# Expert counts as a row on every partition, and their running sums by accumulating VectorE passes

## What is computed

```python
x = x + gnn(layernorm(x), adj, ...)          # dense attention, masked by adj
...
logits = xf @ Wr + br                        # 2048 x 64
topk_logits, topk_idx = jax.lax.top_k(logits, 2)
gates = jax.nn.softmax(topk_logits, axis=1)
combine = zeros((T, E)).at[arange(T)[:, None], topk_idx].add(gates)
for e in range(64):
    h = relu(xf @ W1[e] + b1[e])             # hidden width 256
    y = h @ W2[e] + b2[e]
    out = out + combine[:, e:e + 1] * y
x = x + out
```

## Time and profile before

| what | us |
|---|---|
| median of 3 runs | 273.82 |
| lowest and highest run | 273.25, 275.77 |
| the profiled execution, span from first to last instruction | 278.2 |
| of it: attention stage, about | 17 to 132 |
| last routing and the plan, about | 132 to 167 |
| expert stage, about | 167 to 262 |

### The profile page before, as it was taken

How to read it: one execution, slowest core, us unless ns; L and a number is a source line. 1 busy time by engine, 2 the same in 40 slices (tenths; PEclk the granted TensorE clock), 3 DMA queues, 4 the chain that set the end, 5 groups by cost and what they waited for, 6 DMA issues and landing times.

```text
span 278.2 us, 6188 instructions
## 1 busy us (share of the span) xinstructions
PE 221.1 (79%) x1849; PEld 211.8 (76%) x1849; DVE 219.3 (79%) x628; ACT 173.6 (62%) x393; POOL 167.4 (60%) x194
## 2 busy tenths in 40 slices
PE   1493998989677878869933369999999999999840
PEld 1263998989677877869933249999999999999740
DVE  6899999999999999998866413889887666666464
ACT  2758777978665868658415025878876777777400
POOL 5770007163788588888667344445888888866600
PEclk9998699999999999979995556999999999999995
DMA  6989744876649607019911122222149710100067
GB/s 157 202 164 171 139 76 75 194 194 184 164 85 252 224 26 294 31 26 375 416 45 48 36 57 57 61 66 72 51 133 319 252 40 31 40 28 24 31 199 262
DMA packets 11119, 36.88 MB, mean 133 GB/s; under 512 B 2256, under 2 KB 2832, under 8 KB 10320
## 3 DMA queue, kind: packets, MB, share of 16 engines
q0 software_dynamic: 5232, 14.98, 24.6%
q1 hardware_dynamic: 5424, 21.11, 21.7%
q10 hardware_dynamic: 432, 0.40, 0.6%
HBM read 39.36 MB, written 5.51 MB: 161 GB/s over the span
## 4 chain that ended last, share of the span: by engine, by line
PE 45%; DVE 33%; issue 9%; DMA 5%; another core or an unknown queue 2%; ACT 1%; POOL 1%; SPq 1%; ACTq 1%; POOLq 0%; DVEq 0%
PE bank L1117 17%; PE bank L1129 15%; DVE arena L721 8%; DVE arena L727 7%; PE bank L1015 4%; PE bank L999 3%; DVE arena L712 3%; DMA arena<-result 2%; DMA xs<-in_x 2%; DVE xs L735 2%; DVE st L738 2%; PE bank L1106 1%; DVE xs L808 1%; DVE idx L758 1%
## 5 line engine op out<-in xcount | busy, mean ns | idle before, releaser
L1015 PE MATMUL bank<-arena 128*128 128x130 f32 x512 | 62.7, 279 | 1.9 <-ACT arena L569 1.9
L1015 PEld LDWEIGHTS bank<-arena 128*128 128x128 f32 x512 | 60.4, 194 | 2.6 <-DVE xs L735 1.5
L1117 PE MATMUL bank<-arena 128*128 x384 | 61.3, 284 | 0.6 <-ACT arena L623 0.5
L1129 PE MATMUL bank<-w2s,arena 128*128 x384 | 59.2, 277 | 0.2 <-issue 0.2
L425 POOL DMA_INDIRECT table<-rows_in,pos x32 | 48.0, 1501 | 11.4 <-issue 8.1
L1117 PEld LDWEIGHTS bank<-arena 128*128 128x128 f32 x384 | 52.0, 197 | 1.4 <-issue 1.3
L1129 PEld LDWEIGHTS bank<-w2s,arena 128*128 128x128 f32 x384 | 51.2, 194 | 0.6 <-issue 0.6
L891 DVE SCALAR_TENSOR_TENSOR arena<-bank,arena 128x128 f32 x96 | 33.6, 350 | 22.2 <-PE bank L1129 15.2
L628 ACT ACTIVATE arena<-bank,arena 128x128 f32<-128x128 f32 x96 | 35.2, 367 | 19.8 <-PE bank L1117 15.4
L999 PE MATMUL bank<-ident,arena 128*128 128x128 f32 x256 | 33.8, 290 | 13.9 <-DVE arena L727 13.9
L999 PEld LDWEIGHTS bank<-ident,arena 128*128 128x128 f32 x256 | 30.5, 149 | 15.1 <-DVE arena L727 15.1
(11 more groups left out here) (193 smaller groups left out, 273.9 us busy)
## 6 DMA issues: line engine op xcount, KB each, us to landing
arena<-in_adj POOLq DMA_DIRECT2D x16, 512.0 KB, 5.4
w2s<-in_w SPq DMA_DIRECT2D x8, 768.0 KB, 4.9
arena<-in_w SPq DMA_DIRECT2D x6, 1024.0 KB
arena<-in_w SPq DMA_DIRECT2D x4, 512.0 KB
w2s<-in_w SPq DMA_DIRECT2D x4, 512.0 KB
xs<-in_x SPq DMA_DIRECT2D x4, 256.0 KB, 6.5
arena<-result SPq DMA_DIRECT2D x2, 512.0 KB, 4.3
arena<-result SPq DMA_DIRECT2D x4, 256.0 KB, 6.1
```

What stands on the lines that cost most here:

```text
L1015: ins = pe.matmul(OB[t % 2][:, 0:D + 2], pt_r[:, t % 2, j, :], h[:, j, :], start=(j == 0), stop=(j == T - 1))
L1117: ins = pe.matmul(hp(p, b), w1u[:, p % UW, P * b:P * b + P], xT_all[:, bass.ds(column, P)], start=True, stop=True)
L1129: ins = pe.matmul(yp(p), hT[:, p % UH, b, :], w2s[:, bass.ds(u, 1), b, :].rearrange("p e d -> p (e d)"), start=(b == 0), stop=(b == HB - 1))
```

## The change

The counts are no longer a column with one partition per expert. PE multiplies `ones` (128 x 128) with each `both` matrix, so that all 128 partitions hold the same row of 64 counts (`tally`, in PSUM bank 0). A first product with `tiny` adds the half. Nine of the ten products need only the groups 0 to 5 and stand ahead of the wait for the last group; the last one stands between that wait and `route_c(6)`.

With the row on every partition, DVE makes the running sums itself. It rounds the row (`paired`, 64 x 64), and passes over it twice, once with a mask of the experts below (`below_f`) and once with those up to this one (`upto_f`). Each pass multiplies and accumulates along the row into one column of `blocks_to`. The three products L1077 to L1079 and the two waits around them are gone. The marks come from `blocks_to` by a few instructions on one or two columns. `place(6)` is split into `gates(6)`, which stays ahead of the plan, and `slots(6)`, which now stands behind the plan's first part. The expert's own count for `pad_at` is picked from the row by a third accumulating pass (`mine`), also behind it. POOL makes the two masks at the start of the kernel with a memset and two selects, in place of three copies.

```diff
             top2(6)
-            place(6)
+            gates(6)
...
             dve.wait_ge(s_tp, 1)
-            dve.tensor_scalar(halves[:, :], M0[0:E, 0:1], 0.5, MAGIC, ALU.mult, ALU.add).then_inc(s_half, 1)
-            dve.tensor_scalar(pad_at[:, :], M0[0:E, 0:1], first_row[:, :], None, ALU.add).then_inc(s_pad, 1)
+            dve.tensor_scalar(paired[:, :], tally[0:E, :], 0.5, MAGIC, ALU.mult, ALU.add).then_inc(s_half, 1)
             dve.wait_ge(s_half, 1)
-            dve.tensor_scalar(edge[0:E, :], halves[:, :], MAGIC, 2.0 / P, ALU.subtract, ALU.mult).then_inc(s_edge, 1)
-            dve.tensor_scalar(c_e, halves[:, :], 2.0, -2.0 * MAGIC, ALU.mult, ALU.add)
-            dve.tensor_scalar(side_e, halves[:, :], 2.0, P - 2.0 * MAGIC, ALU.mult, ALU.add)
-            dve.tensor_scalar(w_e, halves[:, :], -1.0, MAGIC + STRIDE // 2, ALU.mult, ALU.add).then_inc(s_num, 1)
-
-            dve.wait_ge(s_tp, 2)
-            dve.tensor_scalar(mark[:, :], ends, MAGIC, None, ALU.add).then_inc(s_mark, 1)
-            dve.wait_ge(s_mark, 1)
+            dve.scalar_tensor_tensor(skip[:, :], paired[:, :], MAGIC, below_f[:, :], ALU.subtract, ALU.mult,
+                                     accum_out=blocks_to[:, 0:1]).then_inc(s_to, 1)
+            dve.wait_ge(s_to, 1)
+            dve.scalar_tensor_tensor(skip[:, :], paired[:, :], MAGIC, upto_f[:, :], ALU.subtract, ALU.mult,
+                                     accum_out=blocks_to[:, 1:2]).then_inc(s_to, 1)
+            dve.wait_ge(s_to, 2)
+            dve.tensor_scalar(last_exact[:, :], blocks_to[:, 1:2], 0.5, (1.0 - P) * 0.5 / P, ALU.mult, ALU.add).then_inc(s_last, 1)
+            dve.tensor_scalar(mark[:, 0:2], blocks_to[:, :], (2.0 - P) * 0.5 / P, MAGIC, ALU.add, ALU.add).then_inc(s_mark, 1)
+            dve.tensor_scalar(c_e, blocks_to[:, 1:2], blocks_to[:, 0:1], float(P), ALU.subtract, ALU.mult).then_inc(s_num, 1)
+            dve.wait_ge(s_last, 1)
+            dve.tensor_scalar(last_g, last_exact[:, :], MAGIC, None, ALU.add).then_inc(s_mark, 1)
             dve.wait_ge(s_num, 1)
-            dve.scalar_tensor_tensor(frac[:, :], last_g, MAGIC, ends[:, 2:3], ALU.subtract, ALU.subtract).then_inc(s_frac, 1)
+            dve.tensor_scalar(w_e, c_e, -0.5, float(STRIDE // 2), ALU.mult, ALU.add).then_inc(s_num, 1)
+            dve.tensor_scalar(side_e, c_e, float(P), None, ALU.add).then_inc(s_num, 1)
+            dve.wait_ge(s_mark, 2)
+            dve.scalar_tensor_tensor(frac[:, :], last_g, MAGIC, last_exact[:, :], ALU.subtract, ALU.subtract).then_inc(s_frac, 1)
...
             dve.tensor_scalar(in_block, part[:, :], frac[:, :], None, ALU.is_le).then_inc(s_where, 1)
 
+            slots(6)
+            dve.wait_ge(s_to, 2)
+            dve.scalar_tensor_tensor(skip[:, :], tally[0:E, :], 1.0, ident[0:E, 0:E], ALU.mult, ALU.mult,
+                                     accum_out=mine[:, :]).then_inc(s_mine, 1)
+            dve.wait_ge(s_mine, 1)
+            dve.tensor_scalar(pad_at[:, :], mine[:, :], first_row[:, :], None, ALU.add).then_inc(s_pad, 1)
+
+            dve.wait_ge(s_num, 3)
             dve.tensor_scalar(r_blk[0:E, :], pair_of, last_e, None, ALU.is_gt)
...
             route_c(5)
-            route_c(6)
...
-            total = earlier(NG)
-            for n, c in enumerate(total):
-                pe.matmul(M0[0:E, 0:1], c, ones[:, 0:1], start=(n == 0), stop=False)
-            pe.matmul(M0[0:E, 0:1], ones_f[0:1, 0:E], half[:, :], start=False, stop=True).then_inc(s_tp, 1)
+            pe.matmul(tally, ones[:, :], tiny[:, :], start=True, stop=False)
+            for c in earlier(NG - 1):
+                pe.matmul(tally, ones[:, :], c, start=False, stop=False)
+            pe.wait_ge(s_both, NG)
+            pe.matmul(tally, ones[:, :], both[:, SLOT[NG - 1], :], start=False, stop=True).then_inc(s_tp, 1)
+            route_c(6)
             pe.wait_ge(s_tri, 1)
-            pe.wait_ge(s_edge, 1)
-            pe.matmul(ends[:, 0:1], before_f[:, :], edge[:, :], start=True, stop=True)
-            pe.matmul(ends[:, 1:2], upto_f[:, :], edge[:, :], start=True, stop=True)
-            pe.matmul(ends[:, 2:3], upto_h[:, :], edge[:, :], start=True, stop=True).then_inc(s_tp, 1)
             pe.wait_ge(s_where, 1)
```

More of the change, by code:

```diff
@@ L120, in build @@
         ones_f = sb("ones_f", [E, P])
-        before_f, upto_f, upto_h = (sb(f"{k}_f", [E + 1, E]) for k in ("before", "upto", "upto_half"))
+        below_f, upto_f, skip = (sb(f"{k}_f", [E, E]) for k in ("below", "upto", "skip"))
+        paired = sb("paired", [E, E])
+        tiny = sb("tiny", [P, E], BF16)
         steps_i = sb("steps_i", [P, TAB + NB + NG2], I32)
@@ L133, in build @@
         sidx = sb("sidx", [P, 1])
-        halves = sb("halves", [E, 1])
+        mine = sb("mine", [E, 1])
+        blocks_to = sb("blocks_to", [E, 2])
+        last_exact = sb("last_exact", [E, 1])
         turn_e = sb("turn_e", [E, 1])
-        edge = sb("edge", [E + 1, 1])
         mark = sb("mark", [E, 3])
@@ L181, in build @@
         LB, RB = [M0] * (NG - 1) + [bank[1]], [M1] * (NG - 1) + [bank[2]]
-        ends, coded, sides, b1_at = bank[0][0:E, 0:3], bank[4][0:1, 0:2 * WORDS], bank[5], bank[3][:, 0:HB * TAB]
+        tally, coded, sides, b1_at = bank[0][:, 0:E], bank[4][0:1, 0:2 * WORDS], bank[5], bank[3][:, 0:HB * TAB]
         d_x = [sem(f"d_x{i}") for i in range(4)]
@@ L428, in _ @@
             load(4)
[L429 to L431 removed]
+            pool.memset(skip[:, :], 2.0 / P).then_inc(s_skip, 1)
+            pool.wait_ge(s_skip, 1)
+            pool.affine_select(out=below_f[:, :], in_=skip[:, :], compare_op=ALU.is_gt, fill=0.0,
+                               base=0, pattern=[[-1, E]], channel_multiplier=1)
+            pool.affine_select(out=upto_f[:, :], in_=skip[:, :], compare_op=ALU.is_ge, fill=0.0,
+                               base=0, pattern=[[-1, E]], channel_multiplier=1)
             pool.tensor_scalar(part[:, :], iota_p[0:E, :], -1.0 / P, ROUND, ALU.mult, ALU.add)
@@ L689, in _ @@
                 dve.memset(radix[E:E + 1, j:j + 1], 64.0 ** j)
[L690 to L694, removed]
+            dve.memset(tiny[:, :], 0.5 / P)
             dve.memset(padrow[:, :, :], 0.0).then_inc(s_set, 1)
-            dve.wait_ge(s_pool, 4)
+            dve.wait_ge(s_pool, 3)
             dve.wait_ge(s_set, 1)
@@ L767, in top2, with gates @@
                 dve.tensor_tensor(both[:, kept(q), :], hot[:, 0, kept(q), :], hot[:, 1, kept(q), :], ALU.add).then_inc(s_both, 1)
-            def place(q):
+            def gates(q):
                 n = SIZE[q]
@@ L776, in place, with slots @@
                 dve.tensor_tensor(gate[:, 1, rows], ge[:, 0:n], gate[:, 0, rows], ALU.mult).then_inc(s_gate, 1)
+            def slots(q):
+                n = SIZE[q]
+                rows = slice(START[q], START[q + 1])
                 dve.wait_ge(s_rk, q + 1)
@@ L786, in place @@
                                          rank[:, :, 0:n], ALU.mult, ALU.add).then_inc(s_pos, 1)
+            def place(q):
+                gates(q)
+                slots(q)
             def base(q):
```

20 lines of the change are left out of this document (10 added, 10 removed).

## The result

| | kernel before | changed kernel |
|---|---|---|
| median, us | 273.81 (15 runs, 272.79 to 275.77) | 275.51 (15 runs, 274.30 to 276.45) |
| ratio to before, 95% interval | | 1.005 [1.0027, 1.0074] |
| span of the profiled execution, us | 278.2 | 273.9 |
| its own time, us | not shown | 275.76 |

The changed kernel is slower by half a per cent, 0.7 to 2.0 us (1.4 by the ratio, 1.70 between the medians). The forecast was 274.2, with 74% for "within 1%". The two spans must not be compared: the one of before holds late turns that its repetition doesn't have (first experiment).

What follows compares the result with a forecast made beforehand. POOL's queue of writes, with landing and gathers, was taken to bound the experts' start. With prompt PE-to-DVE turns, 0.3 for the later first product plus 0.1 for slower writes on 273.82 gave 274.2 us (58%), range 269.5 to 275.6.

Steps and rivals of the forecast that it cites:

- late turns: Waits from PE to DVE ahead of L841, L850 and group 4's L779 in the first trace: 2.55, 2.20 and 1.05 us.
- The late turns are not in the runs: PE-to-DVE turns: 5.8 us of lateness belongs to the profiled execution only; without it the first L1117 starts at 162.1.
- The plan's chain, 2.4 us: DVE from the counts to s_where: 2.4 us (1.8 to 3.4), s_where 5.9 earlier than in the first trace.
- The writes slip by 1.1: POOL's last writes wait for the last s_pos at 152.7, though POOL is free at 151.6.
- 0.7 of it is hidden by ACT: Start of the expert stage: ACT's 0.7 us of slack takes up part of the slip of POOL's writes.
- the 0.3 of the sum: First expert product L1117: at 162.4 in place of 162.1, so 0.3 us later.
- 0.1 for writes beside DVE's plan: POOL's last writes, now beside DVE's plan, add 0.1 us (median write 1026 ns, best 957).
- the 6.2 us: Skill rule: a profile's total lies 6.2 us above the reported time; by it the runs would be 272.0, late waits included.
- What gives or takes in this stage shifts the end one for one: Stage between 141 and 168 us: its gains or losses shift the expert stage and the end by the same amount.
- may differ by a microsecond: PE's clock in the expert stage: its return may differ by a microsecond, counted in the forecast's own range 273.2 to 275.4.
- That late turns were in the runs: Two rivals on PE-to-DVE waits: 269.6 us if tally comes promptly (14%), 271.9 us if it is late too (18%).
- The third rival: slots(6) behind the plan becomes the bound through the last s_pos; 276.6 us with counts 2.4 late; chance 8%.

Runs made afterwards that it cites:

- first experiment: The kernel before, unchanged, run and profiled once more: 273.86 us, ratio 0.9996; the profiled execution took 272.53 us with a span of 270.6.
- the two experiments that close or narrow POOL's gap: Changed kernel with the last group's places ahead of the plan again, 274.48 us; changed kernel with the padding write ahead of the last tile's two writes, 274.71 us.
- the ten transposes: Kernel before with ten extra PE transposes, result unused, ahead of its first take: 274.60 us, ratio 1.0023.
- the padding first: Changed kernel with mine and pad_at ahead of the marks and POOL's padding write ahead of the last tile's two writes: 274.71 us, ratio 1.0026.
- the places first: Changed kernel with the places of the last group (L781 to L790) ahead of the plan again: 274.48 us, ratio 1.0021.
- the kernel before with its loads first: Kernel before with PE's register loads ahead of its last plan products, b1p in another bank and copied later: 276.93 us, ratio 1.0108.
- the changed kernel with transposes: Changed kernel with seventeen extra PE transposes, result unused, ahead of its first take: 274.82 us, ratio 1.0037.
- the last kernel with its loads first: Changed kernel with places ahead of the plan, PE's register loads ahead of its last plan products, one POOL write ahead of tile 14's rstd: 276.40 us, ratio 1.0089.
- the kernel before with its queue earlier: Kernel before with one tile 10 write ahead of tile 14's rstd and ACT's b1p copy behind its first w1 copies: 273.98 us, ratio 0.9993.

## Why the prediction was right, and which term was off

- *The late turns are not in the runs.* Right, as far as it can be seen: the repeated profile, of a run of 272.53 us, has none of them, and its first product comes 21.55 behind tile 15's residual, where I had 162.1 - 141.1 = 21.0.
- *The plan's chain, 2.4 us.* Right: 2.16. Over PE, with the prompt turns of the repeated profile, it is 2.36, so the passes gain 0.2 us; most of the 5.9 us that the prediction read from the first profile were its late turns.
- *The writes slip by 1.1.* Right in the main: 1.04, and the two experiments that close or narrow POOL's gap give back 1.03 and 0.80 us. The 1.1 counts from the moment when POOL is free; between the prediction's own starts (padding at 155.25 against 154.4) lie 0.85, and its later times go by that.
- *0.7 of it is hidden by ACT.* The size is off (the prediction's own times give 0.55), and the cover is another one. In the kernel before the first take starts at 159.74, 5.06 behind the end of L872 at 154.68; the register loads last about that long (5.05 with the ten transposes, which need no gather; 5.2 when moved). Its gather was issued at 156.37; with the 2.94 us from issue to take of the changed kernel (158.02 to 160.96) it was there at 159.31, an estimate. So PE's loads hid some 0.43 of the slip. The experts start 0.68 later, against the 0.3 of the sum. The first product came at 162.66, where I had 162.4.
- *0.1 for writes beside DVE's plan.* Wrong by that much: 0.96 us each, as the others. With that, the rule of the Trainium skill, "SBUF — State Buffer", section "Who interferes with whom", that VectorE can keep GpSimd from writing its descriptors, shows no trace in these two writes. The long writes of the earlier trace rows lie in the attention stage (2.23 us at 122.81 and 2.94 at 125.35 in the repeated profile); what held them up was not tested. Nor do the runs show the 6.2 us of the Trainium skill, "Runtime: NRT & Kernel Launch", section "The ~15µs preamble/postamble breakdown": where a run's time and span are both given, the time lies above the span, by 1.86 us in the changed kernel (275.76 and 273.9). These spans end with the last instruction, so the total that the section speaks of is not among the numbers here.
- *What gives or takes in this stage shifts the end one for one.* This is the step that failed. By the table the end follows the start of the experts by half, and the return of the clock by the other half. I had kept the clock for the range ("may differ by a microsecond") and left it out of the sum. In the two profiles it is the larger part: 3.74 us later, worth 1.9, beside 0.34 for the start. Of the 1.70 in the medians the start alone would so explain 0.34. How much of the rest is the clock's isn't measured: the timed runs have no trace, and the whole has an interval of 0.7 to 2.0.
- *Rivals.* That late turns were in the runs is refuted: no gain came (269.6 or 271.9 was forecast for it), and the run that was profiled again has none. The third rival named the right place (the last `s_pos` feeds POOL's last writes); it needed a late `tally`, which didn't come.

Open: why the clock returns 3.7 us later when the experts start 0.68 later. Two windows show the stretch at the lower level, in the repeated kernel before and in the changed one:

```profile
142.95:163.40 20.45, 12.14 (x83) 9.91 (x84) 9.02 (x52) 7.59 (x15) 13.57 (x15) 0.50 0.18 55
144.00:167.85 23.85, 13.96 (x91) 12.15 (x92) 10.85 (x60) 9.35 (x20) 14.27 (x15) 0.50 0.20 58
```

It ran from 142.93 to 163.41 and from 143.97 to 167.86. On the table's scale it began 0.33 later and lasted 23.9 us in place of 20.5. In the fourteen profiles this stretch has one of three lengths: 20.5 us in seven, 23.9 in six, 27.3 in the kernel before as first shown. So in these profiles the clock's term came as a jump and did not grow with the delay. What decides on the jump isn't shown. In the repeated kernel before PE worked without a break from 159.74 on, and the clock was back at 163.41. In the changed kernel it began at 160.96, paused 0.53 between its two takes, and the clock was back at 167.86; with the padding first it began at 159.63, paused 0.63, and got it at 166.76. With the places first it paused 0.37 and got it at 164.02. The pause alone doesn't explain it: in the kernel before with its loads first PE worked from 161.49 with one pause of 0.33, and the clock was back at 170.17. A kernel that closes the pause alone wasn't tried.

## What to carry to other kernels

Before a wait is shortened, look at what the waiting work feeds and what else that needs: here the plan was 2.6 us ahead of a queue of writes, so the saved turn (0.2 us, with turns as prompt as in the repeated profile) was worth nothing, and what was moved behind the plan to get it was a feeder of that queue. When a stage starts PE from a low clock, the sum must have two terms, the start and the point at which the clock is back. And one profiled execution can hold waits that its repetition doesn't have; compare its span with the runs before anything is built on them.

## What the runs showed of the hardware

- Loading the 48 words of the pair table into PE's registers takes 5.0 to 5.2 us, from the write of the words to PE's next instruction (5.03 in the changed kernel with transposes, 5.21 in the last kernel with its loads first). No row of the profile shows it, and products issued before it run beside it. The repeated profile puts the wait of the first take (2.67 us) down to the gather, which by the estimate above had landed; with the transposes the same wait (2.66) is put down to "issue".
- In this stage a write of 128 rows mostly takes POOL 0.96 us and a step 1.26, beside DVE's plan too (1.06 for the last write in the repeated profile), and the first gather starts 2.05 or 2.06 us after the padding's issue is over, in all but one (2.27) of the profiles in which that gather waits for the padding.
- The granted clock also drops for a while in the attention stage in some executions (0.50 from 120.2 to 127.0 in the profile of the kernel before with its queue earlier). There the residual of tile 15 came at 142.52, against 139.72: part of the spread of the runs lies ahead of the stage that the change touches.
